# Attention scores in float32 pieces: q and k as two float32r pieces in three slots, two heads in the two row halves of the TensorE array

## The chip, the cores and the metric

The kernel runs on one core of a Trainium2 chip. The metric is the device time of one execution in microseconds; a kernel's figure is the median of its runs. A profiled execution of the same program gives a trace of every engine: PE (TensorE matmul), PEld (its weight loads), DVE (VectorE), ACT (ScalarE), POOL (GpSimd), SP (SyncE, which here only issues DMAs), and of the DMA queues.

## What is computed

One block of a transformer on x [16, 128, 256] in float32: 2048 tokens, a cross attention with 16 heads of 16 dimensions, then a mixture of 8 experts (top 2) with a shared expert. Cut to what matters:

```python
def _L0_xattn_ref(x, y, pad_mask, Wq, Wkv):        # x is the layernorm of the input
    d = C // H                                      # 16 heads, d = 16
    q = (x @ Wq.T).reshape(B, N, H, d).transpose(0, 2, 1, 3)
    kv = (y @ Wkv.T).reshape(B, N2, 2, H, d).transpose(2, 0, 3, 1, 4)
    k, v = (kv[0], kv[1])
    attn = jnp.einsum('bhnd,bhmd->bhnm', q * d ** -0.5, k)
    attn = jnp.where(pad_mask[:, None, :, None], attn, jnp.float32(-1000000000.0))
    attn = jax.nn.softmax(attn, axis=-1)
    return jnp.einsum('bhnm,bhmd->bhnd', attn, v).transpose(0, 2, 1, 3).reshape(B, N, C)

x = x + jnp.tanh(g_xattn[0]) * _L0_xattn_ref(_layernorm(x), ctx_768, mask, Wq, Wkv)
x = x + jnp.tanh(g_ffn[0]) * _L0_ffn_ref(_layernorm(x), router, fc1, fc2, gate, up, down)
```

The router's choice of experts is discrete, so the attention is kept close to float32 accuracy. That is why q and k are split into pieces whose products are summed.

## The kernel before, in words

The 16 batches are worked on in G = 8 groups of two (j = 0, 1), 256 tokens each. A software pipeline over steps s runs the stages of several groups beside each other; each engine has its own program, written out by hand in one order, and semaphores join them. After the attention (to about 160 us) come the shared expert's first half, the 39 tiles of the expert loop and the shared expert's second half; these stages are not touched.

**Making the stacks.** For a group, PE computes k (`keys`, L1354) and q (`queries`, L1367) into one PSUM bank, 128 rows by 2 x 256 columns. A value is split into three bfloat16 pieces: ACT copies the first out of PSUM (`first`, L615), DVE subtracts it from the whole (`rest`, L929), ACT rounds the rest to the second (`second`, L619), POOL subtracts that from the rest (`third`, L518). DMAs then copy pieces into the stacks `q_st` and `k_st`: a head's row slots are 6 x 16 = 96 partitions, each slot holding the piece that `K_ROWS` and `Q_ROWS` name, so that one matmul of 96 rows sums the six products that count. A stack's DMA is 128 KB, 12 of them a group: SP issues q's (L373) and the second and third pieces of k (L366), POOL those of k's first piece (L527) once the stack is free.

**Scores.** `scores` (L1407) makes eight heads at a time, 128 queries by 128 keys each, into the two PSUM banks `ps_s`. DVE takes the maxima over them (`maxima`, L935); the next eight heads wait for that. `pieces` (L943 to L947) splits the negated maxima of 16 heads into three bfloat16 pieces in four small operations, PE transposes them (`max_t`, L1423, 48 columns), ACT copies them (L644) and SP's DMA (L381) puts them into three more rows of the q stack, against rows of ones in the k stack. `scores_t` (L1440) then makes the transposed scores minus the maxima with 99 rows, ACT takes the exponential (L650), and `values` (L1456) multiplies by v: four heads lie side by side in column tiles of 32, in plain float32.

**Around them.** PE transposes tokens (L1378, L1465, L1480), projects v (L1388) and runs the router (L1492). DVE has besides the normalized output (`attended`), the residual, the second layernorm (`norm2`, L978), which `tokens_t` (L1480) waits for, and the routing (`places`, `weights`, L1024 to L1055). POOL has two powers a step (L495) and the indirect DMAs that dispatch rows (L510).

A step of the pipeline is one turn of the loop `for s in range(2, G + 2)`, with four groups of eight matmuls of `scores`, four of `scores_t`, and all the rest once for each stage. The code shown carries the line numbers that the rows name.

## Time and profile before

| | us |
|---|---|
| median of 3 runs | 339.99 (339.44 to 340.58) |
| the profiled execution: its span | 337.4 |
| PE busy in that span | 311.1 |
| DVE, ACT, POOL busy | 244.2, 170.2, 129.8 |

A median is 2.6 us over the span, which is what lies around the span. A busy PE is not a PE at its peak: matmuls are pipelined, so a matmul's duration is mostly latency, and what a row of equal matmuls costs is the distance between their starts. That is (time of the row minus the duration of one) / (count minus 1).

### The profile page before, as it was taken

Reading aid. Unit: us, or ns where it says so; the run is one execution under the profiler, and the core shown is the slowest. Engines: PE = TensorE matmul, PEld = TensorE weight load, DVE = VectorE, ACT = ScalarE, POOL = GpSimd, SP = SyncE. Lnnn points to the kernel's source line nnn. Section 1 sums busy time; section 2 is a strip of 40 time slices with the busy share of each in tenths; the row PEclk is TensorE's granted clock in tenths of the full one; section 3 lists DMA queues with packets and bytes.
Section 4 is the critical chain, followed back from the end, with each engine's and each line's share of the span. In section 5 each row is a group of like instructions: output and inputs, shape, how many; then the busy total and the mean of one; then the engine's idle time right before and its main releaser. Section 6 shows DMA issues by size and latency. Waiting matters only on the chain.

```text
span 337.4 us, 8068 instructions
## 1 busy us (share of the span) xinstructions
PE 311.1 (92%) x2505; PEld 255.6 (76%) x2505; DVE 244.2 (72%) x725; ACT 170.2 (50%) x322; POOL 129.8 (38%) x151
## 2 busy tenths in 40 slices
PE   8868989999899976768999999999999999999986
PEld 8756767778678865655556588888888888988875
DVE  5566587798989897787699836766676666643795
ACT  2533767677676662565880516444444444424131
POOL 4741223132374826337740262834334334331000
PEclk9967999999999996979999999999999999999999
DMA  8896595855567564312253002233333233203951
GB/s 227 264 238 166 157 266 171 202 178 158 184 180 212 145 204 146 110 50 79 96 168 98 0 20 64 89 111 102 101 97 105 81 97 100 71 30 95 416 176 62
DMA packets 33061, 46.52 MB, mean 138 GB/s; under 512 B 5471, under 2 KB 27107, under 8 KB 32514
## 3 DMA queue, kind: packets, MB, share of 16 engines
q1 hardware_dynamic: 24994, 26.15, 27.5%
q0 software_dynamic: 4320, 10.92, 9.9%
q10 hardware_dynamic: 3712, 8.98, 8.2%
q8 instruction: 22, 0.36, 0.5%
q14 instruction: 13, 0.11, 0.1%
HBM read 21.55 MB, written 12.62 MB: 101 GB/s over the span
## 4 chain that ended last, share of the span: by engine, by line
PE 60%; DVE 15%; issue 9%; DMA 6%; POOL 4%; ACT 2%; SPq 2%; POOLq 0%; DVEq 0%
PE ps L1674 26%; PE ps L1340 4%; DVE mx L935 4%; PE ps L1388 3%; DVE x_all L1299 3%; PE ps L1407 3%; PE ps L1724 3%; PE ps L1646 3%; POOL dispatched L510 2%; PE ps L1367 2%; PE ps L1543 2%; PE ps L1354 2%; PE ps L1666 2%; PE ps L1552 2%; PE ps L1537 2%
## 5 line engine op out<-in xcount | busy, mean ns | idle before, releaser
L566 POOL DMA_INDIRECT expert_rows<-v_s,slot_u x39 | 38.3, 982 | 62.1 <-ACT v_s L840 46.8
L935 DVE TENSOR_REDUCE mx<-ps 128x8 f32<-128x1024 f32 x32 | 39.1, 1222 | 14.8 <-PE ps L1407 13.9
L650 ACT ACTIVATE probs<-ps 128x1024 f32<-128x1024 f32 x32 | 32.6, 1019 | 12.1 <-PE ps L1440 12.1
L1249 DVE TENSOR_TENSOR act<-ps,sil 128x256 f32<-128x256 f32 x39 | 16.6, 425 | 29.1 <-ACT sil L833 29.0
L833 ACT ACTIVATE sil<-ps 128x256 f32<-128x256 f32 x39 | 15.0, 385 | 39.5 <-PE ps L1674 39.3
L1674 PE MATMUL ps<-fc_hi,xs_hi 128*128 x78 | 34.2, 438 | 0.0
L518 POOL TENSOR_TENSOR work<-work 128x512 bf16<-128x512 f32 x16 | 18.5, 1154 | 35.6 <-ACT work L619 35.4
L1674 PE MATMUL ps<-fc_lo,xs_hi 128*128 x78 | 30.9, 396 | 0.0
L1674 PE MATMUL ps<-fc_hi,xs_lo 128*128 x78 | 30.6, 393 | 0.0
L840 ACT ACTIVATE v_s<-ps,wt 128x256 f32<-128x256 f32 x39 | 18.5, 475 | 19.3 <-PE ps L1674 19.3
L1407 PE MATMUL ps<-stacks 96*128 96x128 bf16 x256 | 21.6, 232 | 5.8 <-DVE mx L935 5.7
L1407 PEld LDWEIGHTS ps<-stacks 96*128 96x128 bf16 x256 | 17.1, 104 | 10.7 <-DVE mx L935 8.2
L1440 PE MATMUL ps<-stacks 99*128 99x128 bf16 x256 | 21.1, 229 | 4.2 <-ACT probs L650 3.2
L1440 PEld LDWEIGHTS ps<-stacks 99*128 99x128 bf16 x256 | 16.9, 102 | 8.5 <-ACT probs L650 4.4
L1674 PE MATMUL ps<-fc_hi,act_hi 128*128 x78 | 22.2, 284 | 0.2
L1674 PE MATMUL ps<-fc_hi,act_lo 128*128 x78 | 22.0, 282 | 0.0
L1674 PE MATMUL ps<-fc_lo,act_hi 128*128 x78 | 22.0, 282 | 0.0
L1456 PE MATMUL ps<-probs,v_s 128*32 128x128 f32 x512 | 19.8, 295 | 0.7 <-DVE att L957 0.6
L1230 DVE TENSOR_TENSOR xs_lo<-ps,xs_hi 128x256 fp32r<-128x256 f32 x39 | 16.1, 414 | 5.2 <-ACT xs_hi L824 5.0
L1258 DVE CAST act_hi<-ps 128x256 fp32r<-128x256 f32 x39 | 16.5, 423 | 3.7 <-PE ps L1724 3.7
L510 POOL DMA_INDIRECT dispatched<-row_s,slot_u x16 | 16.0, 1002 | 7.4 <-issue 4.1
L495 POOL TENSOR_TENSOR rs<-ve,mhalf 128x1 f32<-128x1 f32 x16 | 9.0, 562 | 22.4 <-DVE ve L968 22.2
(219 smaller groups left out, 826.2 us busy)
## 6 DMA issues: line engine op xcount, KB each, us to landing
stacks<-work SPq DMA_DIRECT2D x75, 128.0 KB, 3.8
xs_in<-dispatched SPq DMA_DIRECT2D x39, 129.0 KB, 2.1
fc_s<-in_fc ACTq DMA_DIRECT2D x8, 512.0 KB, 3.7
stacks<-work POOLq DMA_DIRECT2D x18, 128.0 KB, 4.2
fc_s<-in_fc ACTq DMA_DIRECT2D x8, 256.0 KB, 4.2
stacks<-expert_rows SPq DMA_DIRECT2D x2, 1024.0 KB, 6.2
probs<-expert_rows SPq DMA_DIRECT2D x2, 1024.0 KB, 11.0
ctx_s<-in_ctx_t SPq DMA_DIRECT2D x8, 192.0 KB, 3.1
```

Source lines behind the costliest of these rows:

```text
L510: nc.gpsimd.indirect_dma_start(xs, bass.IndirectOffsetOnAxis(slot_u[:, g, m:m + 1], 0), rows_of[g][:, m, :], None, bounds_check=NULL_ROW + ...
L518: nc.gpsimd.tensor_tensor(out[:, 2, :], rest, out[:, 1, :], ALU.subtract).then_inc(ready, 1)
L566: nc.gpsimd.indirect_dma_start(ys, bass.IndirectOffsetOnAxis(dst_u[:, r:r + 1], 0), y_out[:, r, :], None, bounds_check=2 * T - 1, oob_is_e ...
L650: nc.scalar.activation(probs[:, 2 * j + h], ps_t, ACT.Exp, scale=HD ** -0.5).then_inc(probs_ok[j][h], 1)
L840: nc.scalar.activation(y_out[:, r, :], ps[:, 5 + r % 2, 0:D], ACT.Copy, scale=wt[:, r:r + 1]).then_inc(y_ok, 1)
L935: nc.vector.reduce_max(mx[:, j, 8 * h:8 * h + 8], ps_s, AX_X).then_inc(max_ok[j][h], 1)
L1249: nc.vector.tensor_tensor(act[:, par], ps[:, 2 + par, FI:2 * FI], sil[:, par], ALU.mult).then_inc(act_ok, 1)
L1258: nc.vector.tensor_copy(act_hi[:, par], whole).then_inc(ahi_ok, 1)
L1407: last = nc.tensor.matmul(ps_s[:, n, :], q_st[at], k_st[at], start=True, stop=True)
L1440: last = nc.tensor.matmul(ps_t[:, n, :], k_st[at], q_st[at], start=True, stop=True)
L1456: last = nc.tensor.matmul(ps_o[row:row + VW, blk:blk + P], v_s[:, g % 2, j, VW * head:VW * head + VW], probs[:, 2 * j + h, n, :], start=Tr ...
L1674: ins = nc.tensor.matmul(out, a, b, start=first and n == 0, stop=last and n == 2)
```

## The change

q and k are split into two float32r pieces instead of three bfloat16 ones. ACT's copy makes the first in float32r, DVE's subtraction the second; `second` on ACT and `third` on POOL are gone. A head then needs three slots of 16 rows (high*high, high*low, low*high): 48 rows. Heads lie in the two row halves of the array, rows 0 to 47 and 64 to 111, and `scores` and `scores_t` take them in turn, n = 0, 1, 2, ... in halves 0, 1, 0, ..., each half into a PSUM bank of its own. The weight columns of Wq and Wk are reordered to match on the host. The maxima are split into two pieces by two operations in place of four; their transpose is a float32 one of 128 columns, and two DMAs, one a half, put the rows in place. The stacks hold float32 and have half as many heads in a row, so a DMA still moves 128 KB, from 64 partitions with 2 KB each and no longer from 128 with 1 KB. The ones of the k stacks are set by memsets of whole buffers (128 x 2048 float32), the first by DVE before its first statistics, the second by POOL, in place of POOL's memset of three rows.

```diff
-K_ROWS = [(0, 0), (0, 1), (0, 2), (1, 3), (1, 4), (2, 5)]
-Q_ROWS = [(0, 0), (0, 3), (0, 5), (1, 1), (1, 4), (2, 2)]
+K_ROWS = [(0, 0), (0, 1), (1, 2)]
+Q_ROWS = [(0, 0), (0, 2), (1, 1)]
...
-        stacks = sb("stacks", [P, 2, 2, HEADS, TG], BF16)
+        stacks = sb("stacks", [P, 2, 2, HEADS // 2, TG], F32R)
...
+        def halves(stack, slot, buf, pieces, p):
+
+            return [(stack[HALF * a + slot:HALF * a + QK:SLOTS, buf].rearrange("p h t -> p (h t)").bitcast(F32),
+                     pieces[HALF * a:HALF * a + HALF, p, :].bitcast(F32)) for a in range(2)]
...
-                sp.dma_start(q_st[PIECES * HD:PIECES * HD + 3, g % 2, :, P * j:P * j + P],
-                             mx_t[:, j, :]).then_inc(rows_in[j], 16)
+                for a in range(2):
+                    rows = q_st[HALF * a + QK:HALF * a + QK + MAXROWS, g % 2, :, P * j:P * j + P].bitcast(F32)
+                    sp.dma_start(rows, mx_t[HEADS * a:HEADS * a + HEADS, j, :].bitcast(F32)).then_inc(rows_in[j], 16)
...
-            nc.gpsimd.memset(k_f[PIECES * HD:PIECES * HD + 3, :], TWO_ONES).then_inc(kones_ok, 1)
-            pool.wait_ge(kones_ok, 1)
-            third(0, kst, k_rest, k_ok[1], k_pc, k_ok[2])
-            third(0, qst, q_rest, q_ok[1], q_pc, q_ok[2])
+            nc.gpsimd.memset(k_f[:, HEADS // 2 * TG:HEADS * TG], 1.0).then_inc(kones_ok, 1)
...
-                nc.vector.tensor_tensor(out, whole, low[:, 0, :], ALU.subtract).then_inc(ready, 1)
+                nc.vector.tensor_tensor(out[:, 1, :], whole, out[:, 0, :].bitcast(F32), ALU.subtract).then_inc(low, 1)
...
+            nc.vector.memset(mx_pc[:, :, :].bitcast(F32), 0.0).then_inc(dve_link, 1)
+            links[0] += 1
+            nc.vector.memset(k_f[:, 0:HEADS // 2 * TG], 1.0).then_inc(kones_ok, 1)
...
                 for n in range(8):
-                    at = (slice(0, PIECES * HD), g % 2, 8 * h + n, slice(P * j, P * j + P))
-                    last = nc.tensor.matmul(ps_s[:, n, :], q_st[at], k_st[at], start=True, stop=True)
+                    a, i = n % 2, n // 2
+                    at = (slice(HALF * a, HALF * a + QK), g % 2, 4 * h + i, slice(P * j, P * j + P))
+                    last = nc.tensor.matmul(ps_s[:, 4 * a + i, :], q_st[at], k_st[at], start=True, stop=True)
...
-                nc.tensor.matmul(ps_m, mx_pc[:, j, :, :].rearrange("p c h -> p (c h)"), ident_b[:, :],
+                nc.tensor.matmul(ps_m, mx_pc[:, j, :].bitcast(F32), ident[:, :],
```

PE's program keeps its order. The other engines' programs become shorter or change their DMAs. DVE, first half of a step, before (a line number is that of each kernel's own file):

```order
L978 TENSOR_SCALAR row_s<-x_all,mv,rs 128x256 x2
L935 TENSOR_REDUCE mx<-ps 128x8
L956 RECIPROCAL rsum<-ps 128x16
L957 TENSOR_TENSOR att<-ps,rsum 128x256
L943 TENSOR_SCALAR mx_pc<-mx 128x16
L944 SCALAR_TENSOR_TENSOR mx_rest<-mx,mx_pc 128x16
L946 CAST mx_pc<-mx_rest 128x16
L947 TENSOR_TENSOR mx_pc<-mx_rest,mx_pc 128x16
L965 TENSOR_TENSOR x_all<-x_all,att 128x256
```

The same place now:

```order
L955 TENSOR_SCALAR row_s<-x_all,mv,rs 128x256 x2
L910 TENSOR_REDUCE mx<-ps 128x2x4
L933 RECIPROCAL rsum<-ps 128x16
L934 TENSOR_TENSOR att<-ps,rsum 128x256
L923 TENSOR_SCALAR mx_pc<-mx 128x2x8
L924 SCALAR_TENSOR_TENSOR mx_pc<-mx,mx_pc 128x2x8
L942 TENSOR_TENSOR x_all<-x_all,att 128x256
```

Two of the four operations between the normalized output and the residual are gone.

POOL from its first memset of the stacks on, before: `work<-work` is `third`, `stacks<-work` the DMAs of k's first piece, `rs` a power.

```order
L533 MEMSET stacks 3x4096
L518 TENSOR_TENSOR work<-work 128x512 x2
L491 TENSOR_TENSOR rs<-ve,mhalf 128x12
L518 TENSOR_TENSOR work<-work 128x512 x3
L527 DMA stacks<-work 16x8x512 x3
L518 TENSOR_TENSOR work<-work 128x512
L495 TENSOR_TENSOR rs<-ve,mhalf 128x1 x2
```

And now:

```order
L526 MEMSET stacks 128x2048
L491 TENSOR_TENSOR rs<-ve,mhalf 128x12
L522 DMA stacks<-k_pc 16x4x512 x4
L495 TENSOR_TENSOR rs<-ve,mhalf 128x1 x2
L522 DMA stacks<-k_pc 16x4x512 x4
```

No arithmetic but the powers is left on POOL in a step, and it issues four DMAs of k's first piece where it issued three.

SP, one step before, from the maxima's rows of j = 0 (`mx_t`) over q's stack to the low pieces of k:

```order
L381 DMA stacks<-mx_t 3x16x128
L373 DMA stacks<-work 16x8x512 x6
L381 DMA stacks<-mx_t 3x16x128
L354 DMA ctx_s<-in_ctx_t 96x2x256
L366 DMA stacks<-work 16x8x512 x3
```

And now:

```order
L388 DMA stacks<-mx_t 2x8x128 x2
L379 DMA stacks<-q_pc 16x4x512 x6
L388 DMA stacks<-mx_t 2x8x128 x2
L357 DMA ctx_s<-in_ctx_t 96x2x256
L372 DMA stacks<-k_pc 16x4x512 x2
```

The rows of the maxima take a second DMA each, and k's low piece one DMA less.

## Rows read from the trace of the kernel before

**Rows 1.** The page, parts 1 and 2: busy us and share; 40 slices in tenths.
```profile
PE 311.1 (92%) x2505; PEld 255.6 (76%) x2505; DVE 244.2 (72%) x725; ACT 170.2 (50%) x322; POOL 129.8 (38%) x151
...
PEclk9967999999999996979999999999999999999999
```

**Rows 2.** Windows of two steps: stretch, us, busy (x) of PE, PEld, DVE, ACT, POOL; clock; DMA.
```profile
74.50:90.80 16.30, 14.93 (x196) 12.88 (x192) 14.93 (x52) 11.31 (x21) 4.99 (x8) 1.00 0.56 165
90.80:106.50 15.70, 14.74 (x182) 12.41 (x182) 14.30 (x37) 11.23 (x19) 9.13 (x11) 1.00 0.68 198
```

**Rows 3.** Timeline of one step, PE: start us, us, engine, line, names xcount [idle before].
```profile
89.96 0.61 PE L1407 MATMUL ps<-stacks 96*128 96x128 bf16 x8
...
90.51 0.24 PE L1423 MATMUL ps<-ident_b,mx_pc 128*48 128x128 bf16 x1
...
90.67 1.08 PE L1456 MATMUL ps<-probs,v_s 128*32 128x128 f32 x32
...
92.50 0.97 PEld L1492 LDWEIGHTS ps<-wr_s,xt_all 128*128 128x128 f32 x8
```

**Rows 4.** Single lines of the kernel: durations ns min/median/max of weight loads and matmuls.
```profile
L1407 PEld LDWEIGHTS ps<-stacks x256: 95/98/151, 20.6 to 141.4; 96*128 96x128 bf16 x128
L1407 PE MATMUL ps<-stacks x256: 217/219/314, 20.8 to 141.5; 96*128 96x128 bf16 x128
...
L1492 PEld LDWEIGHTS ps<-wr_s,xt_all x64: 186/192/192, 60.3 to 162.3; 128*128 128x128 f32 x64
```

**Rows 5.** Timeline of the end of the kernel, PE: float32r matmuls of 256 and 512 columns.
```profile
320.66 0.28 PE L1674 MATMUL ps<-down_hi,hid_hi 128*128 128x256 f32 x1
320.78 0.28 PE L1674 MATMUL ps<-down_lo,hid_hi 128*128 128x256 f32 x1
...
322.77 0.39 PE L1674 MATMUL ps<-xt_hi,up_hi 128*128 128x512 f32 x1
323.00 0.39 PE L1674 MATMUL ps<-xt_lo,up_hi 128*128 128x512 f32 x1
```

**Rows 6.** Timeline: DVE operations beside POOL's `third`, and one without it.
```profile
93.51 1.05 DVE L1055 TENSOR_SCALAR dest_f<-dest_f 128x8 f32<-128x8 f32 x1
...
101.24 1.66 DVE L978 TENSOR_SCALAR row_h<-x_all,mv,rs 128x256 f32<-128x256 f32 x2
101.27 1.16 POOL L518 TENSOR_TENSOR work<-work 128x512 bf16<-128x512 f32 x1 [0.48 <-ACT work L619]
...
118.81 0.73 DVE L978 TENSOR_SCALAR row_s<-x_all,mv,rs 128x256 f32<-128x256 f32 x2 [0.27 <-issue]
```

**Rows 7.** Waits over the whole span: engine, line, for what: us, times, longest.
```profile
PEld ps L1407 <- DVE mx L935: 8.2, 10, 2.2
...
PEld ps L1423 <- DVE mx_pc L947: 3.8, 3, 1.9
...
PEld ps L1480 <- DVE row_s L978: 2.4, 3, 1.6
...
PEld ps L1480 <- DVE row_h L978: 1.6, 2, 1.3
```

**Rows 8.** Timeline, the rows of the maxima early in the attention, and who waits for them.
```profile
43.16 0.77 SPq L381 DMA_DIRECT2D stacks<-mx_t  x1
...
48.52 0.62 PE L1440 MATMUL ps<-stacks 99*128 99x128 bf16 x8 [0.96 <-DMA stacks<-mx_t]
```

**Rows 9.** Timeline of the start: DVE's memset, its first statistics, the long ones.
```profile
1.56 1.76 DVE L1057 MEMSET v_s<- 128x2048 f32 x1 [0.38 <-issue]
...
4.50 0.75 DVE L897 BATCH_NORM_STATS2 st<-x_all 128x6 f32<-128x256 f32 x2 [0.94 <-DMA x_all<-in_x]
...
14.03 4.01 DVE L897 BATCH_NORM_STATS2 st<-x_all 128x6 f32<-128x256 f32 x12
```

**Rows 10.** Timeline about 130 us: half clock, and what PE waited for.
```profile
129.29 0.30 PE L1423 MATMUL ps<-ident_b,mx_pc 128*48 128x128 bf16 x1 [1.73 <-DVE mx_pc L947]
...
131.69 1.06 PE L1407 MATMUL ps<-stacks 96*128 96x128 bf16 x8
```

155 lines of the change are left out of this document (66 added, 89 removed).

## The prediction, made before the changed kernel ran

> **What bounds the kernel now.** I read the page's busy shares first: PE 92%, DVE 72%, ACT 50%, POOL 38% [rows 1]. The change touches only the attention, so the question is what sets the length of one of its steps. The windows of two whole steps answer it: in 16.3 and 15.7 us PE is busy 14.9 and 14.7, DVE 14.9 and 14.3, ACT 11.2 [rows 2]. PE and DVE are both nearly full, and they hand work to each other: DVE's maxima wait for eight heads of scores, the next eight for the maxima. From the trace of the second step I counted what PE's work takes back to back, by the distance of starts: about 14.2 us, so 1.5 us of a step is waiting. A gain must come out of those waits or out of PE's own work; anything that PE gets on top comes out in full. From 160 us on nothing is changed, so the attention's gain or loss arrives at the end as it is.
>
> **PE: the eight matmuls of a group.** In bfloat16 eight take 0.61 us with 0.22 for the last one's duration: (0.61 - 0.22) / 7 = 0.056 us from start to start, 0.45 for eight [rows 3, 4]. The new ones are float32r, 48 or 50 rows, 128 columns, on half the array; the trace has none. Bounds for one:
> - Float32r on the whole array: 256 columns start every 0.12 us, 512 every 0.23 [rows 5]. Streaming thus scales with the columns, plus 0.01, and 128 columns would take 0.06 to 0.07.
> - A float32 weight load of 128 columns lasts 0.19 us against 0.098 in bfloat16 [rows 4]. The router's matmuls have only 8 columns to stream, so their loads alone set the pace: (0.97 - 0.19) / 7 = 0.111 us each [rows 3]. That is above 0.07, so a load, not the streaming, bounds a float32r matmul of 128 columns. In a row, eight would take 8 x 0.111 = 0.89 us.
> - Two halves at once: the only packed matmuls in the trace are the column tiles of `values`. There 32 matmul instructions of 128 columns in plain float32 take 1.08 us [rows 3]; less about 0.27 for the last, that is 8 rounds of four, 0.11 a round, so four neighbours load and stream at the same time. If two row halves do so as well, a pair takes 0.111 and eight take 4 x 0.111 = 0.44.
>
> So a group costs between 0.44 (halves beside each other) and 0.89 (one after the other), against 0.45. I take 0.44, since the one packed row of this trace shows loads and streams of neighbours in parallel. Over 64 groups this term is 0; its other end is 64 x 0.44 = +28 us. Below 0.44 I see no way, since the load's 0.111 is measured.
>
> The rows of weight loads are what a rule of the Trainium skill describes ("TensorE: Matmul & The Clock Gate", Weight-path perf modes): a fast weight load needs 128 columns and a type that is not FP32. By that rule, leaving bfloat16 gives the fast load up, and the trace agrees, 0.098 against 0.19 us. The same page puts a plain load at the columns over 1.2 GHz, 107 ns for 128; by it, an estimate, the sum would come out like that with the measured 0.111.
>
> **PE: changing the tiling.** In the order of PE's program the row of half-array matmuls now stands between full-array work. The trace shows what such a change costs. The last matmul of L1407 starts at 89.96 + 0.61 - 0.22 = 90.35, that of L1423, with 48 columns, at 90.51, and the column tiles of L1456 at 90.67: 0.16 us each, where the next start in one tiling would be at 0.056 [rows 3]. So 0.10 a change. Before, a step has 7 (L1423 twice in and out, or on to L1456; L1456 twice). Now L1423 is a full transpose, and a step has 13: in and out of half rows around six stretches (four of them bordering full work on both sides), and the column tiles. Six more at 0.10 are 0.6; one float32 load after the 48-column transpose that is no longer held up gives 0.1 back. 0.5 a step, 8 steps: **+4.0 us**. Bounds: 0, if PE was to wait there anyway, to +5.
>
> Here the Trainium skill speaks against the change ("TensorEngine Tiling (Array Packing)", Key Properties): changing the tiling mode, and not just the tile, drains the array. The 0.16 against 0.056 us agrees. Without that rule and those rows the sum would be 4 us lower.
>
> The transposes of maxima become float32 with 128 columns. Others of that kind start 0.11 apart (four in 0.60 with 0.27 for the last), 0.05 over the old one: 16 x 0.05 = **+0.8**.
>
> **DVE.** Two of four small operations of `pieces` go, about 0.2 us each with their links, twice a step: 0.8 us of a step. More hangs on POOL. Beside `third`, DVE's operations stretch: the two of L978 took 1.66 with it and 0.73 without; a tiny L1055 took 1.05, whose shortest instance is 0.17 [rows 6]. Twice a step up to 0.9 goes. But DVE's freed time counts only where PE waits for it. PE's waits of that kind: for `norm2` 2.4 + 1.6 us, for the pieces of maxima 3.8, for the maxima themselves 8.2 [rows 7]. I take off 3.5 of the first (the stretch of L978, and of `places` ahead of it, is nearly all of it), 2.5 of the second, and 0.8 of the third, where the reduction's own 1.2 us has to pass anyway. With 0.5 for ACT, which was held up by the third piece's DMA when it wanted the next copy: **-7.3 us**. Bounds: -3 to -10. What is late next there: the reduction after each eight heads, and PE itself.
>
> **ACT and POOL.** `second` is 0.6 us twice a step, `third` 1.15 twice. Both engines have 4 us and more free in a step [rows 2], so by themselves these are worth nothing; their use is above. The chain from PSUM to stacks loses two links, but SP issues as many DMAs, and q's last one starts when SP gets to it, about when it does now. POOL issues 4 for 3 at 0.55: +0.55 us on k's first piece, wanted some 4 us later: 0.
>
> **DMA.** The stacks' bytes stay, in half as many, larger packets: 0 or a little better. The rows of maxima need a second DMA, which stands 0.75 us behind the first on SP, ahead of q's six DMAs. For j = 1 the old landing leaves room. For j = 0 it took from 43.16 to 47.5 in an early step with PE waiting 0.96 for it [rows 8]: **+0.3**, bounds 0 and +2 (three steps at 0.7). Behind the second DMA, q's stack lands up to 0.7 later, in the same bound.
>
> **The start.** DVE sets 128 x 2048 ones before its first statistics. The same size took 1.76 us; DVE then had 0.94 of waiting left [rows 9]. About 1.1 is exposed and runs through the norms to the long statistics at 14.03, whose end leads to the first maxima; less the chain's own shortening (no `second` between the copies): **+0.6**, bounds -0.5 to +1.2.
>
> **The clock.** The granted clock falls to half in three places, by the digits 6 7, 6 and 7 [rows 1]. At 130 us it fell after PE had waited 1.73 us for the pieces of maxima, and eight matmuls took 1.06 for 0.61 [rows 10]. With the wait shortened, part of some 7 us at half clock goes: **-1.0**, bounds -2.5 to 0.
>
> **The sum.** 0 + 4.0 + 0.8 - 7.3 + 0.3 + 0.6 - 1.0 = -2.6. On the span of 337.4 that is 334.8; with the 2.6 around it, against the median of 340.0: **337.4 us**.
>
> **The rivals.**
> 1. *The halves don't run beside each other* (slower). The place is each group of `scores` and `scores_t`; it holds if weight loads into the two row halves queue, or if float32r of 128 columns streams at half the pace of 256 or less. For it: no row shows packed rows or float32r this short. Against: the column tiles. Price +28, of which PE's remaining waits for DVE and ACT, about 5 us, take some: 337.4 + 28 - 5 = 360. It decides from a pair at 0.12 us upward: a group then costs 0.48 to 0.49, 64 x 0.04 = 2.6 us more, and the gain is gone; at 0.15 the kernel is already some 7 us slower than the forecast, 4 slower than before.
> 2. *The tiling changes eat the gain.* PE's waits shrink only by 3, because the next one, for the reduction, ends later than the one removed; the rest as in the sum: +1.7, 341.7; with a saving of 5, 339.7. Rows 7 speak for it in that the largest wait stays.
> 3. *Everything hides.* The changes of tiling fall into waits and DVE's 10 us count: -2.6 - 4 - 2.7 = -9.3, 330.7. Against: PE has only 1.5 us of waiting a step.
>
> **How the numbers follow.** The forecast has 0.52, of which 0.05 end within 0.3% of before; rival 1 0.24; rival 2 0.16, half within 0.3% and half above; rival 3 0.08. Under 0.3%, 1 us, is what a measurement can't tell from no change. Faster: 0.47 + 0.08 + 0.01 (the good end of rival 2) = 0.56; same 0.05 + 0.07 = 0.12; slower 0.24 + 0.08 = 0.32. The forecast's own range is 333 to 340. The cases of both signs being likely, the range that should hold 8 in 10 has to take in rival 1: 331 to 362.
>
> **What would show it.** Groups of L1407's and L1440's successors at 0.6 us for eight with starts in pairs: the main step is right; at 1.0 or more, rival 1. From a group to full-array work 0.16 us: the tiling term. L978's successor at 0.73 for two everywhere and no wait of L1480's successor for it: the DVE term. First statistics at 5.6 us. A DVE busy near 12.5 us a step beside a PE that hardly waits would confirm that PE alone bounds. The forecast is wrong if PE's starts in a pair are further apart than in the column tiles, or if PE waits for the second DMA of the maxima in every step.

## The result, and the profile after

The changed kernel is slower. The median of its four runs is **365.31 us** (358.86 to 371.80), against 339.83 (339.44 to 340.58) for the kernel before on the same chip. The ratio of the fast runs (358.86 and 362.80 here; a run more than 1.5% above the fastest of its kernel is left out as slow) is 1.062, 95% interval 1.056 to 1.069. A second series of the unchanged file, on another chip, gave 358.98 (357.77 to 367.32) against 340.29, ratio 1.054 (1.050 to 1.058); I had expected 359 to 372 us of it. The forecast was 337.4. The first series' profiled execution (span 370.0 us) was the slowest of its four; the second's (356.7) lies at its median, so sums are made from that one.

The page of the second series, parts 1 and 2; it answers to [rows 1]:

```profile
PE 330.8 (93%) x2505; PEld 268.5 (75%) x2505; DVE 233.8 (66%) x695; ACT 161.7 (45%) x306; POOL 112.4 (32%) x139
...
PEclk9996997599999999555999999999999999999999
```

And the clock's digits of the first series:

```profile
PEclk9985555999999976755579999999999999999999
```

DVE's busy time fell by 10.4 us, ACT's by 8.5, POOL's by 17.4, as intended. PE's rose by 19.7, and the span by 19.3. The digits 5 to 7 say where: the granted clock was half (1.2 for 2.4 GHz) for 6.8, 13.7 and 27.3 us, 47.8 in all, against 10.2 + 6.9 + 3.4 = 20.5 before; in the first series for 37.6 + 10.2 + 37.6 = 85.4. It is the largest single difference of the traces. For the second series I had expected 65 to 90 us of it, so 47.8 was a miss.

Not all of it is the clock. Here are windows of two whole steps at full clock, from `queries` to `queries`: of the second series (us, PE busy (x), clock, DMA), and then the same two of the first (us, PE, PEld, DVE, ACT, POOL busy, clock, DMA). They answer to [rows 2].

```profile
84.67:100.97 16.30, 16.18 (x195) 1.00 0.61 166
100.97:116.70 15.73, 15.68 (x180) 1.00 0.70 195
```

```profile
88.11:105.03 16.92, 16.22 (x194) 13.26 (x193) 13.25 (x47) 10.23 (x18) 3.16 (x6) 1.00 0.57 159
105.03:120.76 15.73, 15.68 (x180) 12.80 (x178) 11.93 (x33) 10.13 (x17) 7.23 (x10) 1.00 0.71 193
```

The kernel before took 16.33 and 15.73 us for these two, counted the same way. So at full clock a step is as long as before, or 0.6 longer in one of the four. But PE is now busy 16.18 of 16.30 and 15.68 of 15.73: its waits are gone, and its own work has filled their place.

The groups themselves, PE's timeline of the second series; it answers to [rows 3]:

```profile
86.60 0.66 PE L1388 MATMUL ps<-stacks 48*128 48x128 f32 x8
87.19 0.33 PE L1404 MATMUL ps<-ident,mx_pc 128*128 128x128 f32 x1
87.45 1.08 PE L1438 MATMUL ps<-probs,v_s 128*32 128x128 f32 x32
```

and the single line's durations (min/median/max ns), which answer to [rows 4]:

```profile
L1388 PEld LDWEIGHTS ps<-stacks x256: 182/188/334, 24.6 to 158.2; 48*128 48x128 f32 x128
L1388 PE MATMUL ps<-stacks x256: 268/273/473, 24.6 to 158.3; 48*128 48x128 f32 x128
```

Eight take 0.66 us with 0.27 for the last. Single records show them in pairs, 3 ns apart, the second pair 0.16 after the first and then one every 0.111 to 0.113. That is the pair that the prediction took, 0.111. Its first open question, whether halves run beside each other, came out as forecast; rival 1 was wrong.

The long stretches at half clock are another matter. Windows of the first series (us, PE, PEld, DVE, ACT and POOL busy, clock, DMA):

```profile
39.00:51.10 12.10, 12.10 (x91) 9.66 (x91) 3.81 (x6) 5.02 (x8) 0.00 (x0) 0.50 0.20 58
51.10:63.10 12.00, 12.00 (x71) 9.19 (x70) 4.67 (x10) 3.66 (x6) 2.70 (x5) 0.50 0.61 178
```

By the records PE had no idle time in these 24.1 us, and the clock stayed at half. As a busy record is mostly latency, I looked at the starts too: no two are more than 0.59 us apart, and the 256-column matmuls of plain float32 follow each other every 0.427, twice their pace at full clock (0.216). That rules out that waits hold the clock there, whatever first brought it down. The Trainium skill ("TensorE: Matmul & The Clock Gate", What's actually happening) says that the clock follows how busy PE has been; here a PE without a gap in its records was not lifted, so records of busy time don't show what the clock follows.

What this costs is seen in the two steps around it. They have the same 302 matmuls in both kernels. First the kernel before (`queries` to `queries`), then the changed kernel, first series:

```profile
24.70:55.97 31.27, 28.48 (x302) 22.83 (x301) 21.48 (x43) 18.56 (x30) 7.52 (x10) 0.92 0.66 179
```

```profile
26.86:71.43 44.57, 43.55 (x302) 33.76 (x300) 19.16 (x37) 16.46 (x26) 3.25 (x6) 0.59 0.45 131
```

These two steps alone are 13.3 us of the 32.6 by which this span is longer, with about 31 us more at half clock (36 for 5) and 1.0 us of idle PE.

Last, who waited for what (us in total, times, longest), to answer [rows 7]:

```profile
PEld ps L1388 <- DMA stacks<-q_pc: 6.8, 4, 3.1
PEld ps L1388 <- DVE mx L910: 5.4, 8, 2.2
...
PEld ps L1422 <- DMA stacks<-mx_t: 3.3, 2, 2.7
```

and PE's own rows of the same view:

```profile
PE ps L1388 <- DMA stacks<-q_pc: 5.9, 4, 2.7
...
PE ps L1422 <- DMA stacks<-mx_t: 2.8, 2, 2.5
PE ps L1422 <- ACT probs L632: 2.5, 2, 1.3
```

The waits for `norm2` are gone and those for the maxima fell from 8.2 to 5.4; new are the stacks. Here is the timeline, SP and PE, around the longest of the maxima's rows, beside [rows 8]:

```profile
48.42 1.39 SPq L388 DMA_DIRECT2D stacks<-mx_t  x2
49.86 3.83 SPq L379 DMA_DIRECT2D stacks<-q_pc  x6
```

```profile
52.22 0.60 PE L1447 MATMUL ps<-ident,ot_s 128*128 128x128 f32 x4
55.30 0.66 PE L1422 MATMUL ps<-stacks 50*128 50x128 f32 x8 [2.48 <-DMA stacks<-mx_t]
...
58.55 1.11 PE L1422 MATMUL ps<-stacks 50*128 50x128 f32 x8
```

The rows, issued from 48.42 on, let PE go at 55.30; at 57.1 the clock was at half, and the next group took 1.11 for 0.66.

### The profile page after: what moved, and what is told of

Read it like the earlier page. It is cut to its first block, busy times and chain, and to the rows that moved or that the text cites. A ratio compares the mean times of both kernels' runs of the same rounds, so it can differ in the third digit from the quotient of the medians.

```text
span 370.0 us, 7986 instructions
## 1 busy us (share of the span) xinstructions
PE 346.8 (94%) x2505; PEld 280.2 (76%) x2505; DVE 234.0 (63%) x695; ACT 161.5 (44%) x306; POOL 112.1 (30%) x139
## 2 busy tenths in 40 slices
DMA packets 27636, 46.58 MB, mean 126 GB/s; under 512 B 4719, under 2 KB 16883, under 8 KB 27090
## 4 chain that ended last, share of the span: by engine, by line
PE 73%; DMA 8%; DVE 7%; SPq 6%; issue 2%; ACT 2%; POOL 0%; DVEq 0%; POOLq 0%; ACTq 0%
PE ps L1656 24%; DMA stacks<-q_pc 6%; PE ps L1388 5%; PE ps L1422 5%; PE ps L1347 5%; PE ps L1438 5%; PE ps L1320 4%; SPq L379 4%; PE ps L1334 3%; PE ps L1447 3%; DVE x_all L1279 3%; PE ps L1519 2%; PE ps L1706 2%; PE ps L1628 2%; PE ps L1525 2%
## 5 line engine op out<-in xcount | busy, mean ns | idle before, releaser
L632 ACT ACTIVATE probs<-ps 128x1024 f32<-128x1024 f32 x32 | 32.6, 1018 | 18.6 <-PE ps L1422 18.6
L1388 PE MATMUL ps<-stacks 48*128 48x128 f32 x256 | 26.4, 337 | 7.8 <-DMA stacks<-q_pc 5.3
L1388 PEld LDWEIGHTS ps<-stacks 48*128 48x128 f32 x256 | 22.1, 242 | 14.7 <-DMA stacks<-q_pc 6.3
L1422 PEld LDWEIGHTS ps<-stacks 50*128 50x128 f32 x256 | 21.9, 240 | 12.5 <-issue 8.4
L1656 PE MATMUL ps<-fc_hi,xs_lo 128*128 x78 | 30.8, 394 | 0.0
L1656 PE MATMUL ps<-fc_lo,xs_hi 128*128 x78 | 30.7, 394 | 0.0
L522 POOL DMA_DIRECT2D stacks<-k_pc x24 | 12.5, 528 | 59.0 <-PE ps L1422 59.0
L1422 PE MATMUL ps<-stacks 50*128 50x128 f32 x256 | 27.1, 343 | 3.4 <-ACT probs L632 2.5
L817 ACT ACTIVATE v_s<-ps,wt 128x256 f32<-128x256 f32 x39 | 18.5, 475 | 19.3 <-PE ps L1656 19.3
L1438 PE MATMUL ps<-probs,v_s 128*32 128x128 f32 x512 | 23.5, 335 | 0.1
L1347 PE MATMUL ps<-work,wq_s 128*128 128x256 f32 x64 | 21.2, 488 | 0.0
L510 POOL DMA_INDIRECT dispatched<-row_s,slot_u x16 | 16.0, 1001 | 10.2 <-issue 6.8
```

The costliest lines, as they stand in the source:

```text
L510: nc.gpsimd.indirect_dma_start(xs, bass.IndirectOffsetOnAxis(slot_u[:, g, m:m + 1], 0), rows_of[g][:, m, :], None, bounds_check=NULL_ROW + ...
L632: nc.scalar.activation(probs[:, 2 * j + h], ps_t, ACT.Exp, scale=HD ** -0.5).then_inc(probs_ok[j][h], 1)
L817: nc.scalar.activation(y_out[:, r, :], ps[:, 5 + r % 2, 0:D], ACT.Copy, scale=wt[:, r:r + 1]).then_inc(y_ok, 1)
L1347: last = nc.tensor.matmul(whole[:, TG * c:TG * c + TG], wq_s[:, k, c, :], xn_t[:, k, :], start=k == 0, stop=k == 1)
L1388: last = nc.tensor.matmul(ps_s[:, 4 * a + i, :], q_st[at], k_st[at], start=True, stop=True)
L1422: last = nc.tensor.matmul(ps_t[:, 4 * a + i, :], k_st[at], q_st[at], start=True, stop=True)
```

## The experiments

Seventeen kernels ran, the second series among them, on five chips. The kernel before measured 339.7 to 340.3 us on three of them and 348.5 to 349.7 on two, so each run is read against its own chip's. "Half clock" is first the sum over the profiled execution, and in brackets the lowest and highest of all runs of that kernel, an estimate from each run's mean granted clock: (1 - clock) x 2 x span. Eight executions of the same changed file lie between 48 and 85 us, so small differences mean nothing, and for some kernels the profiled execution is at one end of the bracket. In the variants marked with a star part of the products is left out.

| | what | us, median (lowest to highest) | before there | half clock, us |
|---|---|---|---|---|
| before | | 339.83 (339.44 to 340.58) | | 20.5 (13 to 41 on the five chips) |
| changed, 1st series | | 365.31 (358.86 to 371.80) | 339.83 | 85.4 (61 to 85) |
| changed, 2nd series | | 358.98 (357.77 to 367.32) | 340.29 | 47.8 (48 to 78) |
| a1_warm | changed, fillers at the start | 381.36 (372.12 to 389.02) | 348.46 | 61.5 (61 to 92) |
| a2_full* | changed, rows 0 to 111 in one | 388.69 (386.29 to 398.17) | 348.46 | 75.2 (76 to 105) |
| a3_serial | changed, one half after the other | 376.12 (366.20 to 380.75) | 348.46 | 88.8 (61 to 96) |
| a4_onehalf* | changed, all in one half | 415.55 (408.39 to 418.86) | 339.66 | 116.0 (116 to 140) |
| a5_fill | changed, fillers before groups | 366.34 (365.98 to 375.32) | 339.94 | 71.8 (51 to 72) |
| f1_actq | changed, a DMA moved to ACT | 369.05 (359.49 to 377.44) | 339.94 | 61.5 (52 to 92) |
| b1_half* | before, 48 rows | 366.31 (361.97 to 373.32) | 348.46 | 75.1 (55 to 82) |
| b2_k64* | before, 64 rows | 353.87 (350.29 to 360.48) | 339.66 | 64.8 (45 to 65) |
| b2_k65* | before, 65 rows | 343.57 (342.33 to 345.58) | 339.66 | 30.8 (27 to 35) |
| c1_drain* | before, one in eight with 64 | 346.13 (344.88 to 347.74) | 339.94 | 30.7 (27 to 31) |
| g1_k65drain* | before, 65 rows, one in eight 64 | 362.23 (349.47 to 363.47) | 340.29 | 71.8 (41 to 72) |
| b4_bfpairs* | before, pairs of 48 and 32 or 35 rows | 390.75 (375.92 to 395.23) | 340.29 | 88.8 (89 to 137) |
| b5_bfpairs* | before, pairs of 48 and 35 rows | 351.64 (348.48 to 354.49) | 349.65 | 61.5 (38 to 61) |
| b3_warm | before, fillers at the start | 342.46 (339.59 to 346.01, and one of 779.61) | 339.66 | 10.2 (10 to 21) |
| d1_nothird* | before, no third piece on POOL | 337.59 (336.05 to 339.14) | 339.94 | 20.5 (13 to 21) |
| h1_dvethird | before, k's third piece on DVE | 340.43 (339.88 to 346.81) | 340.29 | 20.5 (20 to 34) |

From run to run of one file, time and half clock move together. A straight line through the eight executions of the changed kernel gives 0.39 us of span for 1 us of half clock; through b1_half, b2_k64 and g1_k65drain it gives 0.36, 0.47 and 0.43. The five shortest of the eight alone give 0.19, so take it as an estimate. On average the eight had 66 us of half clock and a span of 361.3; on the line, 20.5 us would be 343.6. By this estimate about 18 of the 24 us of loss go with the clock, and 6 with the rest.

### Do the halves run beside each other, and does order matter?

**a4_onehalf**

```diff
-                    at = (slice(HALF * a, HALF * a + QK), g % 2, 4 * h + i, slice(P * j, P * j + P))
+                    at = (slice(0, QK), g % 2, 4 * h + i, slice(P * j, P * j + P))
```

> The changed kernel with all eight heads of a group in row half 0 (the second half's heads are left out and the first half's computed twice), so that nothing can run beside anything. If a pair's two loads and streams really run at the same time, matmuls of one half must start 0.11 us apart, not 0.055, and eight take about 1.05 us for 0.66: 64 x 0.42 = +27 us of PE's work, of which 5 fall into waits: 385 to 392 us with the clock as it is in the changed kernel. If a half alone can take a 48-row float32r matmul every 0.055 us, halves were no gain and the time stays within 1% of the changed kernel. On the clock, theory R (less array work a time lowers it): half clock at least as long as with full-array pieces (about 80 us). Theory S: PE waits less for others, so the clock falls for less than 60 us.

Measured: 415.55 us, ratio 1.227 (1.219 to 1.235); the shortest of the four runs, 408.39, would give 1.202. A group in PE's timeline, at full clock:

```profile
65.56 1.05 PE L1388 MATMUL ps<-stacks 48*128 48x128 f32 x8
```

(1.05 - 0.27) / 7 = 0.111 us from start to start, the figure of [rows 3] for a load-bound float32 matmul. So a half alone goes no faster, and the pairs of the changed kernel are worth a real 0.4 us a group. The median is 24 to 31 us above what was expected from PE's work and the changed kernel's clock, with 116 us at half clock, as theory R had it and not S.

**a3_serial**

```diff
-                    a, i = n % 2, n // 2
+                    a, i = n // 4, n % 4
```

> The changed kernel with the eight heads in the order of halves, four in the first half and then four in the second, so that a matmul's neighbour is nearly always in its own half. If the pairs' 0.11 us comes from loads and streams of the two halves beside each other, each group costs (8 - 1) x 0.111 = 0.78 us more or less in place of 0.44, +22 to +28 us on the changed kernel at the full clock: 380 to 395 us. If the order does not matter (hardware pairs them anyway, or the pairing is not what sets the pace): 358 to 370 us as the changed kernel.

Measured: 376.12 us beside 348.46, which lies between the two ranges and, with 61 to 96 us of half clock, decides nothing. The groups do; they are as short as with alternating halves:

```profile
64.19 0.67 PE L1388 MATMUL ps<-stacks 48*128 48x128 f32 x8 [0.22 <-DMA stacks<-q_pc]
```

Started in order, four matmuls of one half at 0.111 each (a4_onehalf) would alone put the second half's first start 0.33 us behind the first. But all eight start within 0.40 us, in pairs 10 to 15 ns apart, and took 0.67 with the last one's duration. So PE takes the second half's matmuls beside the first's. Here the Trainium skill ("TensorE: Matmul & The Clock Gate", The mechanism) states the opposite, that matmuls start and end strictly in program order; by the starts this is not so here, and the measurement decides, for matmuls on different row halves.

**a2_full**

```diff
-                    at = (slice(HALF * a, HALF * a + QK), g % 2, 4 * h + i, slice(P * j, P * j + P))
+                    at = (slice(0, HALF + QK), g % 2, 4 * h + i, slice(P * j, P * j + P))
```

> The changed kernel with rows 0 to 111 in each matmul of the scores and the transposed scores, the full array in place of a half. Each adds up two heads, and the maxima's rows of the second half are left out, so the scores are not the reference's; q's stacks are zeroed at the start by POOL. No tiling changes, no pairs: each group of eight costs 8 x 0.111 = 0.89 us for 0.45, +28 us, and -4 for the tiling changes. Theory F: the clock is as in the kernel before, mean 0.96 or more, and the time about 340 - 3 - 4 + 28 = 360 us. Theory S: q's stacks come as late as in the changed kernel, so the clock falls as often and stays down as long: mean 0.90, 375 us or more.

Measured: 388.69 us, ratio 1.113 (1.105 to 1.121). A group:

```profile
63.25 1.06 PE L1391 MATMUL ps<-stacks 112*128 112x128 f32 x8
```

Full-array float32r at 0.112 a matmul, whose groups change no tiling, and still 75 us of half clock, 20.5 of them (131.4 to 151.9) over a PE without a gap. So in float32r the clock suffers even where the groups leave the tiling alone. Theory F is out. That the array is without a stream for half of the time (128 columns at 2.4 GHz are 0.053 us, in 0.112) may be why, but no run shows it. Theory S said 375 us or more at a mean clock of 0.90, and 388.69 at 0.901 fits it; what speaks against stalls alone is the next group of runs.

### What brings the clock down: stalls, DMAs, rows, or changes of tiling?

**a1_warm** (90 bfloat16 fillers ahead of the first scores; the start's fall was taken to come from a stall of 2 us there)

```diff
+            warm(90)
```

> The changed kernel with 90 more small bfloat16 matmuls of ones on the whole array before the first scores (5.0 us of PE at the full clock, some 3 of them beyond the wait that is there). Theory F (form): the clock falls at a stall, and comes back late because packed half-array matmuls do not lift it as full-array work does. With no stall at 23.8 us the half clock from 25.5 to 63.1 us does not come, or comes shorter: 345 to 355 us, mean clock 0.93 or more. Theory S (stalls alone): the same here. Rival N: the clock falls anyway at the next short wait (for the first maxima) and stays down as long: 362 to 370 us, mean clock about 0.90.

Measured: 381.36 (372.12 to 389.02) beside 348.46, above both expectations. The early fall went, and 61.5 us at half clock came later, between 106 and 188 us:

```profile
PEclk9999999999976679555589999999999999999999
```

A stall can start a fall; removing one does not keep the clock up.

**b1_half**

```diff
-                    at = (slice(0, PIECES * HD), g % 2, 8 * h + n, slice(P * j, P * j + P))
+                    at = (slice(0, 48), g % 2, 8 * h + n, slice(P * j, P * j + P))
```

(and the same in `scores_t`, as in the next four)

> The kernel before with only rows 0 to 47 in the scores and the transposed scores: three of the six products and the maxima's rows are left out, so the scores are not the reference's. Bfloat16, the pace of 0.056 us, half the array, no pairs; all DMAs and other engines as before. It has the 6 more tiling changes a step, nothing else of the change. Tiling changes alone: 340 + 4 to 5 = 344 to 345 us at the mean clock of before, 0.97. Theory F in its wide form (half-array work, whatever its type, does not hold or lift the clock): mean clock under 0.95 and 350 us or more. If float32r or the pairs are needed for it: 0.96 or more.

Measured: 366.31 us, ratio 1.047 (1.039 to 1.055), 75 us at half clock. This is the run that turned the study. DMAs, DVE, ACT and POOL are as before, its groups have a matmul every 0.056 us, and nothing is float32r. It lost 17.9 us beside its own kernel before, where the change lost 25.5 and 18.7: matmuls on half the array, with the changes of tiling that they bring, are enough for most of the loss.

**b2_k64** and **b2_k65** (64 and 65 rows: the half array with its changes of tiling, and the full array without)

```diff
-                    at = (slice(0, PIECES * HD), g % 2, 8 * h + n, slice(P * j, P * j + P))
+                    at = (slice(0, 64), g % 2, 8 * h + n, slice(P * j, P * j + P))
```

> The kernel before, with only rows 0 to 63 of the stacks in scores and scores_t (some products and the maxima's rows are left out): bfloat16, one row half of the array, nothing beside it, and so the same changes of tiling as the changed kernel. Eight should take 0.61 us as before, and each change between half array and full array or column tiles about 0.10 us, +4 to +5 us over the attention at full clock. Theory R (the clock falls because the scores use fewer rows of the array): 64 rows lie between 48 (366.3 us) and 99 (before), so half clock for 30 to 70 us and 350 to 365 us. Theory T (the changes of tiling, which drain the array, are what the clock answers to): as with 48 rows, 362 to 368, and 65 rows come out near the kernel before. Theory S (only stalls lower the clock): +4 to +5 us, no new half clock.

> The kernel before, with rows 0 to 64 of the stacks in scores and scores_t: one row more than the run with 64, but on the full array, so without the changes of tiling. Some products and the maxima's rows are left out; nothing else differs. Theory R (rows): like the run with 64 rows in half clock, within 10 us of it, and less the 4 to 5 us of the changes of tiling. Theory T (changes of tiling): within 1% of the kernel before and its half clock of about 20 us. Theory S (stalls): within 1% of the kernel before too, or 1 to 3 us under it, as scores_t waits for no rows of maxima by data, only by semaphore.

Measured: 64 rows 353.87 us, ratio 1.034 (1.027 to 1.041); 65 rows 343.57, 1.014 (1.008 to 1.020). The clock's digits, 64 rows and then 65:

```profile
PEclk9985569999999998555599999999999999999999
```

```profile
PEclk9967999999999995857999999999999999999999
```

That 64 rows change the tiling and 65 don't, the traces show at full clock: from a group's last matmul to the router's next one it is 0.056 us before and with 65 rows, and 0.146 with 64. One row more is worth 10 us. Fewer rows alone (65 for 96) cost 3.9 us and 10 us more of half clock; theory R, rows alone, is out. Theories S and T both had 65 rows within 1% of before; it was 1.4%, with 27 to 35 us of half clock in its four runs where the kernel before had 14 to 27 and once 34.

**c1_drain**

```diff
-                    at = (slice(0, PIECES * HD), g % 2, 8 * h + n, slice(P * j, P * j + P))
+                    at = (slice(0, 64 if n == 7 else PIECES * HD), g % 2, 8 * h + n, slice(P * j, P * j + P))
```

> The kernel before, with rows 0 to 63 alone in the last of the eight matmuls of each group of scores and scores_t (part of that head's products and its maxima's rows are left out); the other seven keep their 96 or 99 rows on the full array. So a group's tiling changes as often as in the run with 64 rows, but seven of eight matmuls are full. Theory T (the changes of tiling bring the clock down): about as much half clock as with 64 rows in all eight (65 us in its profile), 350 to 356 us. Theory U (a half array in use for the whole group brings it down): close to the kernel before in half clock, 20 to 35 us, and only the changes' own price of 4 to 6 us: 342 to 347 us.

Measured: 346.13 us, ratio 1.018 (1.014 to 1.021), 30.7 us at half clock. The changes of tiling cost 6.2 us, at the top of what theory U said, and by themselves only 10 us more of half clock. There are more of them than the expectation has: every group changes into its last matmul and out again, which the trace has as 20 and 19 changes in two steps, where 64 rows in all eight have 14 and 13 (neighbouring groups share one) and the kernel before 7.

**g1_k65drain**

```diff
-                    at = (slice(0, PIECES * HD), g % 2, 8 * h + n, slice(P * j, P * j + P))
+                    at = (slice(0, 64 if n == 7 else 65), g % 2, 8 * h + n, slice(P * j, P * j + P))
```

> The kernel before, with rows 0 to 64 in seven of a group's eight matmuls and rows 0 to 63 in the last (the other products and the maxima's rows are left out): the rows of the run with 65 and the changes of tiling of the run with 64 together, but the half array in use for one matmul in eight only. Theory V (fewer rows and draining each take a part, and add up): half clock of 55 to 75 us as with 64 rows, 349 to 356 us. Theory U (the half array in use for the whole group is what counts): half clock of 30 to 45 us, 344 to 350 us.

Measured: 362.23 us, four runs (349.47 to 363.47), 71.8 us at half clock. A window of it:

```profile
34.10:54.60 20.50, 20.50 (x117) 15.10 (x115) 6.84 (x18) 8.00 (x12) 3.80 (x5) 0.50 0.49 145
```

The four runs don't agree. Three took 361.6 to 363.5 us with 71 or 72 us of half clock, which is theory V's, while the times are above both theories'; the fourth took 349.47 with 41. Rows alone had added some 10 us of half clock, changes of tiling alone some 10. The fourth run is what the two give when they are added (20.5 + 10 + 10), and it fits theory U; in the other three they bring about 50 together. So fewer rows and changes of tiling seem to compound in most executions, but one of four doesn't show it, and the runs don't decide between U and V. As this kernel has 6 changes of tiling a step more than the one with 64 rows, it doesn't show either that the half array's use is without effect. What it does show is the changed kernel's picture once more, PE busy 20.50 us of 20.50 at half clock, here with no float32r in the kernel's attention.

**b4_bfpairs** and **b5_bfpairs** (bfloat16, in the two halves in turn)

```diff
-                    at = (slice(0, PIECES * HD), g % 2, 8 * h + n, slice(P * j, P * j + P))
-                    last = nc.tensor.matmul(ps_s[:, n, :], q_st[at], k_st[at], start=True, stop=True)
+                    at = (slice(64, 99) if n % 2 else slice(0, 48), g % 2, 8 * h + n, slice(P * j, P * j + P))
+                    last = nc.tensor.matmul(ps_s[:, 4 * (n % 2) + n // 2, :], q_st[at], k_st[at], start=True, stop=True)
```

> The kernel before in bfloat16, whose eight matmuls of a group take turns between rows 0 to 47 and rows 64 to 95 (98 for scores_t) of its stacks, each row half into a PSUM bank of its own; part of each head's products is left out. It packs the array as the changed kernel does, with fast loads and a full pace of streaming in each half. If the halves run beside each other at bfloat16's own pace, a pair starts every 0.056 us, eight take 0.39 for 0.61, and 64 x 0.22 = 14 us of PE's work go against 4 to 5 for the changes of tiling; the time follows only as far as DVE (14.3 to 14.9 us of a step) lets it. For the clock, theory U' (what counts is how much of the array works for how much of the time) expects less half clock than with rows 0 to 47 alone (68 us), but more than before, as PE now waits more: 340 to 356 us. If two halves can't run beside each other in bfloat16, a matmul starts every 0.056 us as before: 358 to 368 us.

Measured: 390.75 us. Two groups of its timeline at full clock:

```profile
99.84 0.40 PE L1440 MATMUL ps<-stacks 48*128 48x128 bf16 x8
100.08 1.32 PE L1407 MATMUL ps<-stacks 48*128 48x128 bf16 x8
```

In `scores` the second half had 32 rows (64 to 95), in `scores_t` 35. With 48 and 35 rows eight take 0.40 us; with 48 and 32 they take 1.32, a start every 0.157. I read this as a smaller tile for 32 rows, so that the tiling changed at each matmul: 0.157 against 0.056 is 0.10 each, the price of a change in [rows 3]. It was a slip of mine. The next run has the larger tile everywhere.

> The kernel before in bfloat16, whose eight matmuls of a group take turns between rows 0 to 47 and rows 64 to 98 of its stacks, in scores too (there rows 64 to 95 were used in the last such run, a smaller tile, so that the tiling changed at every matmul and eight took 1.32 us). Part of each head's products is left out, and the three rows of maxima are set to 0 at the start. In scores_t such eight already took 0.40 us, a pair every 0.055. Expected: both kinds of group at 0.39 to 0.40 us for eight, 64 x 0.21 = 13 us of PE's work less, 4 to 5 more for the changes of tiling. Theory W (half clock comes with PE's work made of few rows and many changes of tiling): half clock of 50 to 80 us like 64 rows on one half, 346 to 360 us in spite of the shorter groups. Rival: with both halves streaming at full pace the array does as much as before in its time, half clock stays at 20 to 35 us, and DVE bounds the steps: 336 to 344 us.

Measured: 351.64 us beside 349.65, ratio 1.005 (1.001 to 1.009). A group, and a whole stretch at full clock:

```profile
77.74 0.40 PE L1412 MATMUL ps<-stacks 48*128 48x128 bf16 x8
```

```profile
86.00:102.00 16.00, 13.71 (x191) 10.64 (x191) 14.70 (x42) 10.56 (x20) 7.54 (x10) 1.00 0.59 176
```

Packed bfloat16 does what packed float32r doesn't: PE is busy 13.7 of 16 us. The profiled execution has 61.5 us of half clock all the same, and is the highest of ten; the others have 38 to 58, at the lower end of theory W's 50 to 80 or below it, and above the rival's 20 to 35. The time, 351.64, is within W's 346 to 360, but on a chip where the kernel before takes 349.65 and not 340, so it speaks for neither. It ends within 0.5% of before: shorter groups pay for the changes of tiling and for the clock, with nothing left over.

**a5_fill** (two bfloat16 fillers ahead of every group of the changed kernel)

```diff
+                for n in range(2):
+                    nc.tensor.matmul(ps_s[:, n, :], ones_b[:, :], ones_b[:, :], start=True, stop=True)
```

> The changed kernel with two bfloat16 fillers of 128 x 128 on the full array ahead of every group of scores and scores_t, into the bank that the group then overwrites: 64 x 2 x 0.056 = 7 us of full-array work more, with the same changes of tiling. Theory U (too little of the array is in use for its time): the half clock shrinks by more than the fillers cost, from about 85 to under 55 us, and the time goes to 352 to 362. Theory T (changes of tiling): half clock as before, the fillers come on top: 368 to 375.

Measured: 366.34 us (365.98 to 375.32), ratio 1.080 (1.077 to 1.084), between the two expectations, with 51 to 62 us of half clock in four runs and 72 in the profiled one: 7 us of fillers came back in part at most. It doesn't tell the two apart.

**f1_actq** (the second half's rows of maxima by ACT's queue)

```diff
-                for a in range(2):
+                for a in range(1):
...
+                sa.wait_ge(maxt_ok[j], g + 1)
+                rows = q_st[HALF + QK:HALF + QK + MAXROWS, g % 2, :, P * j:P * j + P].bitcast(F32)
+                sa.dma_start(rows, mx_t[HEADS:HEADS + HEADS, j, :].bitcast(F32)).then_inc(rows_in[j], 16)
```

> The changed kernel with the second half's DMA of the maxima's rows issued from ACT, behind its copy, and no longer from SP ahead of q's stack. If the late q stack (waits of about 5 us in all in the changed kernel) and the clock that falls behind such waits are the cause of the loss, 5 us come off by the waits alone and 10 to 25 with the clock: 340 to 358 us. If the cause is what PE's work is made of, q's stack lands 0.7 us earlier a step, half clock stays at 70 to 90 us, and the time within 1.5% of the changed kernel: 358 to 368.

Measured: 369.05 us (359.49 to 377.44). PE's waits in it:

```profile
PE ps L1428 <- ACT probs L638: 7.3, 8, 2.2
...
PE ps L1394 <- DMA stacks<-q_pc: 0.8, 1, 0.8
```

The wait for q's stack fell from 5.9 to 0.8, and the one for ACT's exponential rose from 2.5 to 7.3, as ACT now waits for its own copy before it issues. Half clock is 61.5 in this execution and 52 to 92 in the four, much as in the changed kernel, and none of the 10 to 25 us came back. So the late stack is not needed for the low clock. But a wait of the same size took its place, so what fewer waits in all would do to the clock, and what the late stack costs by itself, this run leaves open.

### The gain that was expected, by itself

**d1_nothird**

```diff
-                nc.gpsimd.tensor_tensor(out[:, 2, :], rest, out[:, 1, :], ALU.subtract).then_inc(ready, 1)
+                w = TG * 2 if g == 0 else 1
+                nc.gpsimd.tensor_tensor(out[:, 2, 0:w], rest[:, 0:w], out[:, 1, 0:w], ALU.subtract).then_inc(ready, 1)
```

> The kernel before, whose POOL computes only one column of the third piece from the second group on (the rest of it is left out); every semaphore, copy and DMA stays. This measures alone what the prediction put at the most of its gain: DVE's operations no longer stretched by POOL. By the prediction's working (3.5 us of the waits for norm2, part of the waits for the pieces) 3.5 to 5 us come off: 335 to 336.5 us. The rival: DVE gets shorter in its records, by 0.9 us twice a step, but PE is the bound and the time stays within 0.5%.

Measured: 337.59 us, ratio 0.992 (0.989 to 0.995): 2.4 us less, below the 3.5 to 5 expected. DVE's operation, and PE's largest wait:

```profile
101.70 0.73 DVE L979 TENSOR_SCALAR row_h<-x_all,mv,rs 128x256 f32<-128x256 f32 x2
```

```profile
PE ps L1408 <- DVE mx L936: 6.9, 9, 3.2
...
PE ps L1481 <- DVE row_s L979: 0.7, 1, 0.7
```

The same two rows of the kernel before are

```profile
PE ps L1407 <- DVE mx L935: 5.7, 9, 2.0
...
PE ps L1480 <- DVE row_s L978: 1.4, 1, 1.4
```

The pair of L979 took 0.73 for the 1.66 of [rows 6], and the wait for it fell from 1.4 to 0.7; the wait for the maxima rose from 5.7 to 6.9. Part of the gain turned into the next wait, as rival 2 had it.

**h1_dvethird** (k's third piece on DVE, after its second maxima)

```diff
+                if live(s - 1) and s > 2:
+                    ve.wait_ge(k_ok[1], s)
+                    ve.wait_ge(kst[(s - 2) % 2], copied(kst, s - 2))
+                    nc.vector.tensor_tensor(k_pc[:, 2, :], k_rest, k_pc[:, 1, :], ALU.subtract).then_inc(k_ok[2], 1)
```

> The kernel before, complete, with the third piece of k (from the third group on) made by DVE after its second maxima of the step, and no longer by POOL beside norm2 of DVE. DVE takes 0.65 us for it and gets back the 0.93 by which POOL stretched it: 0.3 us a step, 2 us in all, and with the shorter waits for norm2 337.5 to 339.5. Rival: the piece then stands ahead of the normalized output and the pieces of the maxima, for which PE waits, and the gain goes: 340 to 342.

Measured: 340.43 us, ratio 1.001 (0.998 to 1.003). The rival held. PE's wait for the maxima went to 8.7 us (9 times) from 5.7 in the kernel before:

```profile
PE ps L1410 <- DVE mx L934: 8.7, 9, 1.4
```

**b3_warm** (the kernel before, fillers in PE's waits of the first 26 us)

```diff
+            warm(18, 3)
...
+            warm(14, 3)
...
+            warm(8, 3)
...
+            warm(30, 3)
```

> The kernel before with fillers (bfloat16 matmuls of 128 x 128 into a free PSUM bank) in PE's waits of the first 20 us: 18 after the first v projection, 14 after the second group's transposes, 8 after the second v projection, 30 after the first eight scores. They cost no wait anybody else sees if they fit, which the trace will show. If the half clock at 19.5 to 29.7 us follows from PE's idle start, it goes, and some 3 to 4 us of the 10 with it: 336 us for 340 (ratio 0.988 to 0.992). If the clock falls there whatever PE did before, the time stays within 0.3% or rises by 1 us.

Measured: 342.46 us, ratio 1.007 (1.004 to 1.010). The windows of the start of it, and of before (us, PE, PEld, DVE, ACT and POOL busy, clock, DMA):

```profile
10.00:26.00 16.00, 13.78 (x128) 11.91 (x127) 9.49 (x38) 6.81 (x12) 9.74 (x6) 1.00 0.81 200
```

```profile
10.00:26.00 16.00, 12.35 (x59) 9.70 (x58) 10.10 (x36) 6.75 (x12) 8.82 (x5) 0.80 0.89 242
```

The half clock of the start went, as expected, and no time with it. The third group of scores started 0.6 us earlier (27.67 for 28.22), and by the seventh step this was gone. In the start PE waits for stacks and DVE, and half clock costs only where PE bounds. I expected 336 and was wrong. The test is not a clean one, though: with the fillers ahead of them the first scores started at 23.31 us, where the kernel before has 20.84, so part of what the clock gave back may have gone there.

No version tried beats the kernel before but d1_nothird, which leaves out part of the computation.

## Why the prediction was wrong, by its steps

**The sum, forecast and measured,** for the second series, span 356.7 against 337.4:

| term | forecast | measured | from |
|---|---|---|---|
| a pair of halves at 0.111 | 0 | 0 | 0.111 to 0.113 |
| changes of tiling, transposes of maxima | +4.8 | about +8.8 | groups and their neighbours, 1.1 a step |
| DVE's and ACT's waits | -7.3 | about -8.8 | steps at full clock as long as before |
| rows of maxima, stacks | +0.3 | about +4 to +7 | the remainder; their waits are 8.7 |
| the start | +0.6 | +1.3 | first `queries` at 11.75 for 10.50 |
| the clock | -1.0 | +11 to +13.7 | 27.3 us more at half clock, 0.39 to 0.5 of them |

Half of the time is an upper end for the clock, since half clock costs nothing where PE waits; the remainder grows by what is taken off it. The clock and the remainder together are 18 of the 19.3 us. In the first series' profile there are 64.9 us more at half clock, by the same two factors 25 to 32 of the 32.6 us. So how much is the clock's and how much the waits' is an estimate; that the clock's is the larger part rests on the two steps shown above and on b1_half and b2_k64, which have none of the changed kernel's DMAs.

**The clock is the step that failed,** in its sign and in its size. I read [rows 10] as: a wait brings the clock down, fewer waits bring it back. The fall does follow waits, in the changed kernel too (2.48 us ahead of the one at 57.1). But what a fall costs is how long it lasts, and that I took for what it was before, 3 to 10 us. In the profile of the kernel before no fall lasts longer; in the changed kernel they last up to 37.6 us, and with few bfloat16 rows and changes of tiling up to 41, where stretches of 17 to 24 us have a PE without a gap (17.0 in b1_half, 20.5 in g1_k65drain, 24.1 here). The bounds I gave, -2.5 to 0, held nothing above zero, though no row of before bore on how the clock would answer to half-array matmuls. It should have had an upper end of its own, and a place among the rivals. The falls also outlast the attention: in the first series the last one runs to 189.4 us, and from the last `scores_t` to the last router matmul, where the change touches nothing on PE, it is 14.3 us for 11.2. So the sentence that the attention's gain or loss arrives at the end as it is was 3 us off there.

**The pairs** were right, and so was the chain of reasoning to them: load-bound, 0.111 us, column tiles as the model.

**The changes of tiling** were right by kind and came out at almost twice the size. From the first start of a group to the full-array start behind it there are 0.59 us (86.60 to 87.19), where 0.44 + 0.10 were forecast: the second pair comes 0.16 behind the first, not 0.11. Per step, counted from start to next start, the eight groups take about 4.6 us for 3.9, and what stands beside them 0.3 to 0.4 more. I had 0.6 a step for 1.1.

**DVE.** The waits did go, and more than forecast: two steps at full clock are as long as before with PE's own work 1.1 us longer. But since PE then had no idle time left, that is all that could be had. That the term came out near its size is in part luck: the waits that I read in [rows 7] as PE's are those of its weight loads. PE's own were 5.7 for the maxima, 2.2 for their pieces and 2.4 for `norm2`, so 3.5 us could not come off the last. And d1_nothird, which takes away only `third`, gained 2.4 us.

**The rows of maxima and q's stack.** I gave +0.3, bounds 0 to 2, from the time that SP needs to issue one more DMA. What came late was the landing: issued at 48.42, in place at 55.30, 6.9 us. [rows 8] have 5.4, from 43.16 to 48.52; the 47.5 of the prediction is where PE's wait began, and so I took the landing for 1 us earlier than it was. The prediction named a wait for this DMA in every step as a sign of being wrong; PE waited for it twice in all. The runs don't show why; f1_actq moved the wait and didn't settle it.

**The rivals.** None of them had the clock. The forecast of 337.4 and its range up to 362 held the second series' median and missed the first's, and where it held it was luck: the upper end was there for halves that run one after the other.

**What stays open:** what the clock answers to. Whether few rows and changes of tiling compound or only add up, what in a float32r row without changes of tiling (a2_full) does the same, and why executions of one file differ by up to 37 us of half clock, the runs don't show.

## What to carry to other kernels

Before PE's work is rearranged into half-array matmuls, price the clock as a term of its own with an open upper end: here 24 to 44 us of extra half clock came from 64 bfloat16 rows on half the array with every other engine's program unchanged, and a cheap run with one slice changed (64 rows in place of 96) would have shown it before the change was written. Look at the granted clock of several runs, not of one profile, since it moves by tens of us from run to run. Half clock costs what it seems only where PE is the bound; at the start of this kernel fillers that removed it gained nothing. A load-bound float32r matmul of 128 columns (0.111 us) makes packing two in the halves a draw with bfloat16 one by one (0.056).
